# Post-norm transformer layer on 8 cores: value products one period behind their exponentials, later divisions, a spread bound and loads moved into pass 6

## Reference

```
Q, K, V = x Wq^T, x Wk^T, x Wv^T            # 16 heads of 64
O = softmax(causal(Q K^T / 8)) V            # online softmax over blocks of 128 keys
x = layernorm(x + O Wo^T)
g, u = x (w_gate/127)^T, x (w_up/127)^T     # hidden 3072, integer weights
x = layernorm(x + (silu(g) * u) (w_down/127)^T)
```

## Time and profile before

| | |
|---|---|
| median of 3 runs | 1427.88 us (1427.81 to 1454.22) |
| profiled execution, its own time | 1426.56 us |
| its span (slowest core) | 1425.5 us; all cores 1423.1 to 1425.5 |
| PE / VectorE / ScalarE busy | 1312.2 / 466.9 / 727.0 us |
| mean granted PE clock, by core | 0.981 to 0.988 |
| attention, to the last evacuation | 828.0 us |
| output projection, to the first gate product | about 828 to 920 us |

### The profile page before, as it was taken

One profiled execution on the slowest core, in us unless ns is written; L12 is line 12 of the kernel. 1 busy time (PEld: TensorE's weight loads), 2 busy tenths in 40 slices (PEclk: granted clock), 3 DMA queues, 4 the chain that ended last, 5 costly groups with the idle time before them and its releaser, 6 DMA issues.

```text
span 1425.5 us, 23549 instructions; the slowest of 8 cores (1423.1 to 1425.5 us)
## 1 busy us (share of the span) xinstructions
PE 1312.2 (92%) x8432; PEld 606.4 (43%) x8432; DVE 466.9 (33%) x854; ACT 727.0 (51%) x809; POOL 97.7 (7%) x190
## 2 busy tenths in 40 slices
PE   5989999999999999998976868799999999999998
PEld 2634434445344344353332334344444444444443
DVE  1433334333443343334231146412222232222222
ACT  0067777777777777777866945511111401131123
POOL 2000000000000000000001100021001101100100
PEclk9999999999999999999987989999999999999999
DMA  9913223323222232222226620085125504432422
GB/s 154 159 33 53 39 53 53 53 46 53 45 48 44 54 53 38 46 39 46 48 31 143 181 67 1 1 297 191 45 81 156 177 7 156 148 105 88 148 74 104
DMA packets 38861, 119.66 MB, mean 84 GB/s; under 512 B 13280, under 2 KB 13280, under 8 KB 36576
## 3 DMA queue, kind: packets, MB, share of 16 engines
q0 software_dynamic: 24096, 100.68, 30.5%
q1 hardware_dynamic: 14656, 17.47, 4.0%
HBM read 145.13 MB, written 27.39 MB: 121 GB/s over the span
## 4 chain that ended last, share of the span: by engine, by line
PE 79%; ACT 5%; issue 5%; DMA 5%; DVE 5%; POOL 0%; DVEq 0%; ACTq 0%; SPq 0%; POOLq 0%
PE ops L565 16%; PE gps L846 12%; PE dps L906 12%; PE ups L852 12%; PE pp L260 8%; PE pp L299 7%; PE sps L517 7%; ACT pt L525 4%; PE pp L278 4%; DMA xb<-xP 3%; PE dps L758 2%; DMA linvd<-rcol 1%; DVE pt L545 1%; DVE ostg L581 1%; DVE sq L328 1%
## 5 line engine op out<-in xcount | busy, mean ns | idle before, releaser
L525 ACT ACTIVATE pt<-sps,cbias 128x1024 bf16<-128x1024 f32 x544 | 578.0, 1115 | 168.6 <-PE sps L517 166.0
L565 PE MATMUL ops<-pt,vbuf 64*65 64x512 bf16 (+3 forms) x2560 | 390.2, 356 | 39.2 <-DVE pt L545 24.6
L858 ACT ACTIVATE sgb<-gps 128x512 bf16<-128x512 f32 x96 | 57.3, 597 | 370.3 <-PE gps L846 370.3
L517 PE MATMUL sps<-qbuf,kbuf 64*128 64x512 bf16 (+3 forms) x1280 | 212.7, 350 | 6.9 <-ACT pt L525 6.5
L565 PEld LDWEIGHTS ops<-pt,vbuf 64*65 64x65 bf16 x2560 | 123.4, 107 | 202.4 <-issue 168.1
L846 PE MATMUL gps<-x1T,wgu 128*128 128x512 bf16 x768 | 182.5, 381 | 0.0
L852 PE MATMUL ups<-x1T,wgu 128*128 128x512 bf16 x768 | 181.4, 379 | 0.0
L906 PE MATMUL dps<-wd,hbuf 128*128 128x512 bf16 x768 | 166.4, 379 | 0.0
L861 DVE SCALAR_TENSOR_TENSOR hbuf<-ups,sgb 128x512 bf16<-128x512 f32 x96 | 66.4, 691 | 267.4 <-PE ups L852 267.4
L260 PE MATMUL pp<-xb,wkb 128*128 128x512 bf16 x512 | 134.2, 385 | 20.5 <-DMA xb<-xP 17.7
L299 PE MATMUL pp<-wvb,xb 128*128 128x256 bf16 x1024 | 132.6, 273 | 10.6 <-DVE vbuf L311 5.4
(11 more groups left out here) (54 smaller groups left out, 555.5 us busy)
## 6 DMA issues: line engine op xcount, KB each, us to landing
wgu<-wgub POOLq DMA_DIRECT2D x96, 512.0 KB, 3.8
wgub<-wguP POOLq DMA_DIRECT2D x24, 512.0 KB, 5.3
xb<-xP POOLq DMA_DIRECT2D x8, 1024.0 KB, 37.0
lb<-linvd SPq DMA_DIRECT2D x32, 256.0 KB, 3.7
x<-xtok POOLq DMA_DIRECT2D x16, 512.0 KB, 4.6
yout<-x SPq DMA_DIRECT2D x15, 512.0 KB, 2.6
wdb<-wdP POOLq DMA_DIRECT2D x12, 512.0 KB, 5.7
wd<-wdb POOLq DMA_DIRECT2D x6, 1024.0 KB, 7.5
```

The lines of the kernel that those rows point to most:

```text
L517: mm = pe.matmul(buf[:, h * 512 + so:h * 512 + so + w], kt[r, kb * 128:kb * 128 + 128], qt[r, g * 512 + q0:g * 512 + q0 + w], start=True, ...
L525: exp_at[j] = s_act.inc(act.activation(pt[j % NPT][:, :], buf[:, :], AF.Exp, bias=cbias[p % 2][:, 0:1]))
L565: mm = pe.matmul(ops[:, h * 512 + q0:h * 512 + q0 + w], vt[r, c0:c0 + 65], pt[j % NPT][r, h * 512 + so:h * 512 + so + w], start=(s["first" ...
L858: gps_free[0] = s_act.inc(act.activation(sgb[j][:, :], gps[:, :], AF.Silu, scale=QS))
```

## The change

- `values` of a period are queued one period later: half 0 of the period before (`fresh`), half 1 of the one before that (`begun`). A period's queue on PE is now: half 1 of `begun`, half 0 of `fresh`, both `scores`, filling. At a unit's start half 0 comes behind the filling, which then holds `AT_END` too. `pt` has 6 buffers instead of 4, `lb` one instead of two.
- `unit_recip` and `unit_scale` are due 8 and 18 steps after `finished`'s period begins, 6 and 13 after a pass's last bank. `finished` itself comes one period later than it did.
- `together` adds `ALONE` = 4 units to the cost of each stage of the bound that stands alone, and `filler_cost` of pass 6 adds 24.
- Output weights are loaded in eight pieces: 2 to 7 in pass 6 (every eighth step), 0 and 1 at the start of pass 7. The weight buffers of the projections are placed so that the pieces lie over those no longer used.
- The residual's tiles are loaded in pass 6: after every second group of keys and its group of queries four of them, three steps apart.

```diff
--- before.py
+++ after.py
@@ -83,7 +83,7 @@
     NPASS = NH // 2
     NTT = TOWN // 128
     NWB = 4
-    NPT = 4
+    NPT = 6
     NOS = 3
     QS = cfg["QSCALE"]
     VW = 4 * 65
@@ -135,8 +135,10 @@
 
         at_b = region(B0)
         ofm = at_b("ofm", [128, NCH * TOWN], BF16)
-        wkb = [at_b(f"wkb{i}", [128, NCH * 128], BF16) for i in range(2)]
-        wqb = [at_b(f"wqb{i}", [128, NCH * 128], BF16) for i in range(2)]
+
+
+        wkq = [at_b(f"wkq{i}", [128, NCH * 128], BF16) for i in range(4)]
+        wkb, wqb = [wkq[2], wkq[0]], [wkq[3], wkq[1]]
         wvb = [at_b(f"wvb{i}", [128, NCH * 256], BF16) for i in range(2)]
         at_b = region(B0 + 32 * KB)
         wob = at_b("wob", [128, NCH * D], BF16)
@@ -156,7 +158,7 @@
         at_d = region(D0)
         pt = [at_d(f"pt{i}", [128, 1024], BF16) for i in range(NPT)]
         ostg = [at_d(f"ostg{i}", [65, 1024], F32) for i in range(NOS)]
-        lb = [at_d(f"lb{i}", [64, 1024], F32) for i in range(2)]
+        lb = [at_d("lb0", [64, 1024], F32)]
         at_d = region(D0)
         hbuf = at_d("hbuf", [128, NHC * 512], BF16)
 
@@ -187,7 +189,7 @@
         s_wv = [Sem(st, nc, f"s_wv{i}") for i in range(2)]
         s_lc = [Sem(st, nc, f"s_lc{i}") for i in range(4)]
         s_lw = [Sem(st, nc, f"s_lw{i}") for i in range(4)]
-        s_lb = [Sem(st, nc, f"s_lb{i}") for i in range(2)]
+        s_lb = [Sem(st, nc, "s_lb0")]
         s_wo = Sem(st, nc, "s_wo")
         s_x1 = [Sem(st, nc, f"s_x1{i}") for i in range(4)]
         s_wg = [Sem(st, nc, f"s_wg{i}") for i in range(NWB)]
@@ -393,6 +395,8 @@
             roots(p)
             yield 0.0
 
+        ALONE = 4.0
+
         def together(groups, stages):
 
             for g in groups:
@@ -401,13 +405,40 @@
                 if cost is not None:
                     yield cost
             for cost in stages:
-                yield cost
+                yield cost + ALONE
+
+        pending = []
+        tick = [0]
+
+
+        pieces = [(wgub[n], wguP[n]) for n in range(NHC)]
+        pieces += [(wdb[:, n * 2 * D:(n + 1) * 2 * D], wdP[:, n * 2 * D:(n + 1) * 2 * D])
+                   for n in range(NHC // 2)]
+
+        def convert_piece():
+            if pieces:
+                to, of = pieces.pop(0)
+                wait(pool, s_pe, s_pe.n)
+                s_cv.inc(pool.dma_start(to, of), 16)
+
+        def wo_load(n):
+            s_wo.inc(pool.dma_start(wob[:, n * D:(n + 1) * D], woP[:, n * D:(n + 1) * D]), 16)
+
+        def x1_load(t, x_done):
+            wait(pool, s_pe, x_done)
+            s_x1[t // 4].inc(pool.dma_start(x1[t][:, :], xtok[t * 128:(t + 1) * 128, :]), 16)
 
         def proj_kq(p):
             for ts in range(NTS):
                 yield from k_group(p, ts)
                 if ts % 2 == 1:
                     yield from q_group(p, ts // 2)
+                    if p == NPASS - 1:
+
+                        for k in range(4):
+                            pending.append((tick[0] + 1 + 3 * k,
+                                            lambda t=2 * ts - 2 + k, n=s_pe.n: x1_load(t, n)))
+                        pending.sort(key=lambda e: e[0])
             if p + 2 < NPASS:
                 wait(pool, s_pe, s_pe.n)
                 load_wk(p + 2)
@@ -432,6 +463,8 @@
             if p + 1 >= NPASS:
                 return 0.0
             cost = 12 * 8 + 5.5
+            if p == NPASS - 2:
+                cost += 6 * ALONE
             if 2 * ((p + 2) // 2) < NPASS:
                 cost += 8 * 16 * 0.52
             return cost
@@ -499,7 +532,6 @@
         pt_at = {}
         pv_at = {}
         evac_at = [0]
-        pending = []
         wo_ready = {}
 
         def scores(j):
@@ -571,7 +603,7 @@
             pv_at[j] = s_pe.inc(mm)
 
         ostg_free = [0] * NOS
-        lb_free = [0, 0]
+        lb_free = [0]
 
         def unit_out(u, j):
 
@@ -592,13 +624,13 @@
             s_lw[i].inc(sp_q.dma_start(
                 linvd[u:u + 1, :].rearrange("o (p f) -> (o p) f", f=8), rcol[i][:, :]), 16)
             wait(sp_q, s_lw[i], s_lw[i].n)
-            k = u % 2
+            k = 0
             wait(sp_q, s_dve, lb_free[k])
             s_lb[k].inc(sp_q.dma_start(
                 lb[k][:, :], linvd[u:u + 1, :].partition_broadcast(64)), 16)
 
         def unit_scale(u):
-            k = u % 2
+            k = 0
             p, g = u // NBANK, u % NBANK
             o = ostg[u % NOS]
             wait(dve, s_lb[k], s_lb[k].n)
@@ -613,24 +645,6 @@
         def settle(now):
             while pending and pending[0][0] <= now:
                 pending.pop(0)[1]()
-
-
-        pieces = [(wgub[n], wguP[n]) for n in range(NHC)]
-        pieces += [(wdb[:, n * 2 * D:(n + 1) * 2 * D], wdP[:, n * 2 * D:(n + 1) * 2 * D])
-                   for n in range(NHC // 2)]
-
-        def convert_piece():
-            if pieces:
-                to, of = pieces.pop(0)
-                wait(pool, s_pe, s_pe.n)
-                s_cv.inc(pool.dma_start(to, of), 16)
-
-        def wo_load(n):
-            s_wo.inc(pool.dma_start(wob[:, n * 2 * D:(n + 1) * 2 * D],
-                                    woP[:, n * 2 * D:(n + 1) * 2 * D]), 16)
-
-        def x1_load(t):
-            s_x1[t // 4].inc(pool.dma_start(x1[t][:, :], xtok[t * 128:(t + 1) * 128, :]), 16)
 
         def look_ahead(j):
 
@@ -652,20 +666,21 @@
             if done["last"]:
                 u = done["unit"]
                 unit_out(u, j)
-                pending.append((j + 6, lambda u=u: unit_recip(u)))
-                pending.append((j + 16, lambda u=u: unit_scale(u)))
+
+
+                late = (6, 13) if done["g"] == NBANK - 1 else (8, 18)
+                pending.append((tick[0] + late[0], lambda u=u: unit_recip(u)))
+                pending.append((tick[0] + late[1], lambda u=u: unit_scale(u)))
                 pending.sort(key=lambda e: e[0])
-            if done["p"] < NPASS - 1:
-                if j % 13 == 12:
-                    convert_piece()
-            else:
-                n = j - (NJ - 68)
-                if n < 8 and n % 2 == 0:
-                    wait(pool, s_pe, s_pe.n)
-                    wo_load(n // 2)
-                elif n >= 8 and n % 3 == 0 and n // 3 - 3 < NTT:
-                    wait(pool, s_pe, s_pe.n)
-                    x1_load(n // 3 - 3)
+            if done["p"] < NPASS - 1 and j % 13 == 12:
+                convert_piece()
+            n = j - (NJ - 136)
+            if 0 <= n < 48 and n % 8 == 2:
+                wait(pool, s_pe, s_pe.n)
+                wo_load(2 + n // 8)
+            if n in (68, 70):
+                wait(pool, s_pe, s_pe.n)
+                wo_load((n - 68) // 2)
 
 
         NJ = len(plan)
@@ -675,18 +690,21 @@
                 periods[-1].append(j)
             else:
                 periods.append([j])
-        periods.append([])
+        periods += [[], []]
 
         AT_END = 7.5
         scores(0)
         scores(1)
-        before = []
+        begun, fresh = [], []
         for n, now in enumerate(periods):
+
+
             heads = n % 2
-            if before:
-
-                wait(pe, s_pe, pv_at[before[-1]])
-            for j in before:
+            tick[0] = now[0] if now else NJ
+            if begun:
+
+                wait(pe, s_pe, pv_at[begun[-1]])
+            for j in begun:
                 values(j, 1, heads)
                 finished(j)
             if now and plan[now[0]]["first"]:
@@ -694,17 +712,22 @@
 
                 steps = len(bank_steps(plan[now[0]]["g"]))
                 share = max(0.0, rate[0] * steps - AT_END) / ((steps + 1) // 2)
+            new_bank = bool(fresh) and plan[fresh[0]]["first"] and fresh[0] > 0
+            if not new_bank:
+                for j in fresh:
+                    values(j, 0, heads)
             for j in now:
                 look_ahead(j + 2)
                 masks(j)
-                if plan[j]["first"] and j > 0:
-                    credit[0] += AT_END
-                    fill(0.1)
-                values(j, 0, heads)
                 settle(j)
+            if new_bank:
+                credit[0] += AT_END
             credit[0] += share
             fill(1.0)
-            before = now
+            if new_bank:
+                for j in fresh:
+                    values(j, 0, heads)
+            begun, fresh = fresh, now
         att_pe = s_pe.n
         att_act = s_act.n
         att_dve = s_dve.n
```

## The result

The changed kernel takes 1.0093 times the time of the kernel before (95% interval 1.0052 to 1.0134): 0.9% slower, where 2.9% faster had been forecast. Its profiled execution took 1439.57 us against 1426.56. (The median of all its executions, 1452.38 us, is higher because in 8 of the 17 one die ran disturbed; the ratio leaves those out.)

The account below looks back on a forecast made before the run. PE was taken to bind the full passes, ScalarE pass 7. Savings of 13 us (full passes), 13.5 (pass 6) and 15 (pass 7) sum to 41.5: 1426.6 - 41.5 + 1.3 = 1386 us, range 1375 to 1405.

Parts of the forecast that it names:

- the second score is not late: Paired scores: ScalarE needs 2.0 us a pair, periods are 2.50 in full passes, 2.15 in pass 6 (at most 0.2 late).
- which I take as equal: Unit starts: one filling stretch falls away, head turns have nothing between; 0.1 to 0.2 us each, four times a pass.
- rival C: Full passes: paired scores give back what the masks gave, 13 us, making 1399 us; chance 0.07.
- The waits removed: Full passes: later value products remove PE's 10.1 us of mask waits and 2.7 of evacuation waits, say 13 us.
- The later divisions: Reciprocals and divisions due later after the evacuation; claimed to change nothing in passes 0 to 5.
- Pass 6, the bound: Spreading the bound's stages removes 4.6 us of waits for squares and the clock's fall; pass 6 takes 78 instead of 91.5 us.
- VectorE may stand at a division up to 5 us: Pass 6 with moved loads: transfers take 16.7 us against 11.5 allowed; after cover, 0 to 2 us inside the 78.
- rival A: Pass 6: the DMA backlog reaches PE, two of three units stall it 3 us beyond cover, clock falls; 1400 us, chance 0.12.
- Pass 7: 68.3 us of exponentials plus about 2.5 for bank changes and clearing: 71 us, 15 less; ends 69 and 77.
- The single broadcast buffer: One lb instead of two: each broadcast waits on SP for the division before; priced at nothing, else 1 or 2 us each.
- Rival B: Pass 7 and end of pass 6: PE's clock stays low, costing 20 us and making 1406 us; chance 0.05.
- D: Slower than before: pass 6 transfer pairs exceed 16.7 us at every unit, units 24 to 27 each lose 11.2; 1431 us, chance 0.03.

Follow-up runs that it names:

- Experiments 1 to 3: Changed kernel with value products between the scores in ordinary periods, filling between them at unit starts, or both: 1418.95, 1418.74 and 1405.99 us.
- experiment 3: Changed kernel with both edits of the order on PE, in ordinary periods and at unit starts; lag, late divisions, spread bound, moved loads kept: 1405.99 us, ratio 0.986.
- 6: Kernel before with later reciprocals and divisions alone, two broadcast buffers kept and loads still in pass 7: 1436.46 us.
- experiment 5: Kernel before with the spread bound alone, 4 units more for each of six stages in pass 6: 1418.62 us.
- 7: Changed kernel with both edits of the order on PE, and output weights and residual loaded in pass 7 again: 1405.5 us.
- 4: Changed kernel with output weights and residual loaded in pass 7 as in the kernel before: 1441.91 us.
- 11: Changed kernel with the gate alone: from unit 24, GpSimd issues nothing between a unit's reciprocal and its broadcast's landing: 1433.82 us.
- 12: Changed kernel with both order edits, thinner loads (residual tiles six steps apart, output weights every 11th step), and the gate from unit 23: median 1397.21 us, ratio 0.9762.
- experiment 9: Changed kernel with both order edits, loads as dense as before the edits, and the gate from unit 24: 1404.56 us, ratio 0.9848.

## Why the prediction was wrong

The forecast of 1386 us was missed by 55 (span 1438.5 where 1384 was implied): 35 in passes 0 to 5, 20 in pass 6, none in pass 7.

- **The step that failed first** is "the second score is not late" in a full pass, with "which I take as equal" for the change of turns. The comparison of means, 2.0 us of ScalarE against a period of 2.50, is right in the middle of a unit (a period of the changed kernel takes as long, 2.43 to 2.50) and wrong at its start, where the periods before are short and PE is ahead. I had the condition written down in rival C, "only stretches with a late first score do", and did not count that there are four such stretches in each pass. It cost 4.3 us a pass by the starts of pass 4, and the turns, priced at 0.1 to 0.2, were 0.32. Rival C had the mechanism, with 13 us where 35 were missed. Experiments 1 to 3 show the cause: scores and turns moved apart again on PE, and nothing else changed, give back 5.2 of 98.8 us.
- **The waits removed** were sized at 13 us. They are gone, but with the order mended they leave 8.6. The wait for a cast of value filling rose from 5.0 to 10.2 us after, and is 11.9 in experiment 3, so a part was handed on to it; the sum of the named waits doesn't close to 8.6, and I haven't settled the rest. The later divisions may be in it: the sum had them at nothing in these passes, and in the kernel before they cost 1.1 us in each (6).
- **Pass 6, the bound.** Forecast 78 us. The spread alone brings 83.8 (experiment 5), with the mended order 81.1 (7), with the paired scores 87.6 (4). The mechanism was right (no wait for squares, granted clock 1.00 in all three), the term mis-sized by 3 us, and the paired scores took 6.5 more: "at most 0.2 us in the second" failed here as well (PE waits 9.7 us for ScalarE in pass 6, 20 times).
- **Pass 6, the loads.** "VectorE may stand at a division up to 5 us" and "4.9 us of one more group" as cover: it stood up to 11.5 us, and PE 7.8. This is rival A, and the row that I had (16.7 us for the pair against 11.5 allowed) was taken for the worst. In pass 6 each of the two transfers can be behind a backlog of its own: the pair whose reciprocals left at 714.66 needed 18.7 us. Shown by 4, 7, 11 and 12.
- **Pass 7** came out at 71.5, with the forecast's 71. Of the gain 12.5 us are the loads' (4); the later divisions, at no price in my sum and meant for the same wait, gave nothing when made alone and cost in the full passes (6). The sign that I had named, divisions without a wait for the broadcast, did not show: one waited 5.3 us, and the pass came out as forecast all the same.
- **The single broadcast buffer**, priced at nothing, cost nothing that shows: in experiments 4 and 7 no division of pass 6 waits for a broadcast.
- **Rival B** did not come: PE's granted clock is 0.98 in pass 7. **D** neither: a pair over its 16.7 us came (18.7), but not at every unit. That the time lies near D's 1431 is chance, since the larger part was lost in the full passes.
- **The rule on queues** that was weighed (the Trainium skill, DMA: Bandwidth & Descriptors, Queues, rings and completion order: each engine takes its queues in turn) does not carry what I concluded from it, that a small transfer passes a backlog. The runs speak against that by 8.8 us for 4 KB, and by the gate, which does nothing but hold bulk loads back: it brings pass 6 to the length without moved loads on six of eight cores in experiment 11, and within 0.3 us of it on all eight in 12, with the thinner loads. Whether the engines take their queues in turn, no run here shows.
- **The range**: C and A were each counted with 13 or 14 us and as alternatives. They were independent, so both could hold at once, and both were sized by one row. Even added, 1413 us, they fall short of what came.

## What to carry to other kernels

With two buffers between two engines, the second of two instructions that each need a buffer, queued back to back, can wait as soon as their engine is ahead. Here it was ahead where periods are short, though not on average: put independent work between them, above all at the borders of units. Small transfers on which an in-order engine waits took long here when bulk loads were issued just ahead of them, though on another queue, so hold the bulk loads back until they have landed and keep the bunches small. Thin loads alone left 9 us on the slowest core and the gate alone 15. But the gate of experiment 12 also begins a unit earlier than that of 9, and no run has the dense loads behind the earlier gate, so that thinning was needed as well isn't shown. Rivals that don't exclude each other must be added, and a wait that is removed must be followed to who is next at the same engine.

## What the runs showed of the hardware

Under a backlog, transfers of different queues landed nearly in their order of issue. From the changed kernel's trace, issue and landing of all eleven from 713 to 737 us (`linvd` and `lcol` 4 KB, `lb` and `wob` 256, `x` and `wdb` 512):

```
713.19 -> 724.11   POOL  wob<-woP
713.71 -> 725.48   POOL  x<-xtok
714.66 -> 723.48   SP    linvd<-rcol
717.14 -> 728.20   POOL  x<-xtok
720.07 -> 733.28   POOL  wdb<-wdP
720.59 -> 733.92   POOL  x<-xtok
722.62 -> 736.37   POOL  wob<-woP
723.14 -> 736.76   POOL  x<-xtok
723.61 -> 733.39   SP    lb<-linvd
723.66 -> 738.89   POOL  x<-xtok
736.81 -> 739.08   SP    lcol<-ostg
```

The broadcast issued at 723.61 lands 0.1 us after the load issued 3.5 us ahead of it, at 720.07; a transfer of 4 KB issued once all but the last load of the backlog have landed (736.81) takes 2.3 us. SP's transfers do pass the last two or three loads ahead of them, not the earlier ones, and size made little difference: 8.8 us for 4 KB, 9.8 for 256 KB. One large transfer ahead is enough. In experiment 7, without any moved load, a conversion of weights issued at 701.83 landed at 710.35 and the broadcast issued at 702.60 at 711.21: 8.6 us, where the other three broadcasts of that pass, with no load just ahead of them, took 3.6 to 3.8.

The cores of one execution differ by up to 15 us in pass 6 (81.1 to 96.1 in experiment 9) wherever loads and broadcasts collide, and by at most 0.3 where no division is held up for long (experiments 4, 5, 7 and 12; 0.9 in the kernel before): with such collisions the slowest core, which is the time, is set by the least lucky of eight.
